# Folding the value and output weights of an attention block into one product per head, and mixing each image's context with 32-column products

## The reference: what is computed

```python
# layer 0, per image; n = 4096 pixels, four memory keys and values
xn = x / norm * g * C ** 0.5                  # norm over the channels
q, k, v = split(einsum('bchw,oc->bohw', xn, w_qkv))
k = concat([mk, k]); v = concat([mv, v])
q = softmax(q, axis=-2) * dh ** -0.5          # over the 32 channels of a head
k = softmax(k, axis=-1)                       # over the pixels
context = einsum('bhdn,bhen->bhde', k, v)
out = einsum('bhde,bhdn->bhen', context, q)
x = x + einsum('bchw,oc->bohw', out, w_out) + b_out
# layer 1
x = x + conv3x3(_gn(x), w3 * m3) + einsum(_gn(x), w1 * ~m3) + b.sum(axis=1)
```

## Time and profile before

| | before |
|---|---|
| median of three runs (lowest, highest) | 2064.62 us (2064.17, 2066.17) |
| the profiled execution, and its span | 2065.06 us, 2063.2 us |
| TensorE busy | 1913.9 us, 93% |
| VectorE busy | 1750.3 us, 85% |
| ScalarE busy, GpSimd busy | 1354.0 us, 1362.4 us |
| mean granted clock of TensorE | 0.983 |
| chain that ended last | TensorE 45%, VectorE 36%, ScalarE 12%, GpSimd 3% |

### The profile page before, as it was taken

One profiled execution on the slowest core, in us unless ns is written; L12 is line 12 of the kernel. 1 busy time (PEld: TensorE's weight loads), 2 busy tenths in 40 slices (PEclk: granted clock), 3 DMA queues, 4 the chain that ended last, 5 costly groups with the idle time before them and its releaser, 6 DMA issues.

```text
span 2063.2 us, 50607 instructions
## 1 busy us (share of the span) xinstructions
PE 1913.9 (93%) x21199; PEld 1013.4 (49%) x21199; DVE 1750.3 (85%) x3144; ACT 1354.0 (66%) x1476; POOL 1362.4 (66%) x737
## 2 busy tenths in 40 slices
PE   2889999999999999999999999999999999999996
PEld 0445445555445555444555544555544555554552
DVE  5689888888988888988888988888988888898863
ACT  2567666767667767667676766676766776766761
POOL 5566666766667766667676667676666676666762
PEclk9789999999999999999999999999999999999997
DMA  5357777887767887667787777778777778876665
GB/s 105 62 127 147 154 149 158 168 169 153 149 154 160 169 168 158 151 148 160 169 158 165 154 152 153 162 164 173 149 151 151 159 168 171 154 151 147 144 136 127
DMA packets 349427, 312.96 MB, mean 152 GB/s; under 512 B 299152, under 2 KB 299920, under 8 KB 341008
## 3 DMA queue, kind: packets, MB, share of 16 engines
q1 hardware_dynamic: 347712, 308.73, 72.1%
q10 hardware_dynamic: 1168, 0.98, 0.2%
q0 software_dynamic: 320, 0.01, 0.0%
HBM read 68.10 MB, written 67.11 MB: 66 GB/s over the span
## 4 chain that ended last, share of the span: by engine, by line
PE 45%; DVE 36%; ACT 12%; POOL 3%; issue 1%; DMA 1%; ACTq 0%; SPq 0%
PE pair_ps L765 8%; DVE km L1114 7%; DVE u L1111 7%; PE pair_ps L802 7%; PE pair_ps L745 5%; DVE image L1166 4%; DVE nrm L1101 4%; DVE parts L1101 3%; PE bank_ps L699 3%; POOL exp_kT_lo L447 3%; PE bank_ps L775 3%; PE pair_ps L768 3%; PE pair_ps L793 3%; DVE part L1100 2%; PE bank_ps L754 2%; PE bank_ps L757 2%
## 5 line engine op out<-in xcount | busy, mean ns | idle before, releaser
L802 PE MATMUL pair_ps<-replicas,w_rep 96*32 96x512 f16 x8192 | 488.9, 383 | 7.9 <-DMA replicas<-yg_lo 7.9
L444 POOL TENSOR_TENSOR u_lo<-u,u_hi 128x1024 f16<-128x1024 f32 x128 | 269.9, 2144 | 270.3 <-ACT u_hi L551 270.3
L447 POOL TENSOR_TENSOR exp_kT_lo<-exp_kT,exp_kT_hi 128x1024 f16<-128x1024 f32 x128 | 300.2, 2354 | 178.9 <-ACT exp_kT_hi L560 178.8
L802 PEld LDWEIGHTS pair_ps<-replicas,w_rep 96*32 96x32 f16 x8192 | 205.8, 96 | 263.2 <-issue 77.8
L450 POOL TENSOR_TENSOR u_lo<-exp_q,u_hi 128x1024 f16<-128x1024 f32 x128 | 272.7, 2143 | 88.8 <-ACT u_hi L566 85.3
L1166 DVE SCALAR_TENSOR_TENSOR image<-pair_ps,image 128x512 f32<-128x512 f32 x256 | 172.5, 682 | 123.5 <-PE pair_ps L802 119.8
L440 POOL TENSOR_SCALAR u<-image,st 128x1024 f32<-128x1024 f32 x128 | 187.4, 1475 | 109.2 <-DVE st L1065 109.2
L551 ACT ACTIVATE u_hi<-u 128x1024 f16<-128x1024 f32 x128 | 130.8, 1045 | 173.3 <-DVE u L1111 173.1
L557 ACT ACTIVATE exp_kT<-pair_ps,zcol 128x1024 f32<-128x1024 f32 x128 | 141.0, 1102 | 144.0 <-PE pair_ps L745 144.0
L566 ACT ACTIVATE u_hi<-exp_q 128x1024 f16<-128x1024 f32 x128 | 135.3, 1057 | 137.1 <-DVE exp_q L1153 130.5
L536 ACT ACTIVATE exp_kT<-u,zcol 128x1024 f32<-128x1024 f32 x128 | 146.0, 1143 | 93.2 <-POOL u L440 92.2
(11 more groups left out here) (179 smaller groups left out, 4716.5 us busy)
## 6 DMA issues: line engine op xcount, KB each, us to landing
image<-in_x SPq DMA_DIRECT2D x256, 256.0 KB, 4.8
out<-image SPq DMA_DIRECT2D x512, 128.0 KB, 2.2
replicas<-yg_hi SPq DMA_DIRECT2D x256, 165.0 KB, 3.9
replicas<-yg_hi SPq DMA_DIRECT2D x256, 107.2 KB, 5.1
replicas<-yg_lo SPq DMA_DIRECT2D x128, 165.0 KB, 4.4
replicas<-yg_lo SPq DMA_DIRECT2D x128, 107.2 KB, 3.8
uT_hi<-u_hi SPq DMA_TRANSPOSE x128, 3.4
uT_lo<-u_lo SPq DMA_TRANSPOSE x128, 3.4
```

The costliest lines, as they stand in the source:

```text
L444: pool.tensor_tensor(px(UL, v), px(U, v), px(UH, v), ALU.subtract).then_inc(ul_ready, 1)
L447: pool.tensor_tensor(KL[:, v % 2], KT[:, v % 2], KH[:, v % 2], ALU.subtract).then_inc(kl_ready, 1)
L802: mm = pe.matmul(conv_ps[32 * r:32 * r + 32, j % 2], w_rep[0:32 * SLOTS, tap, r], rep[:, j * ROWS + dy:(j + 1) * ROWS + dy, dx:dx + SIDE], ...
```

## The change

Per image: `weigh_context` no longer scales; it sums z, copies the context and takes the reciprocal. `turn_context` transposes the unscaled context and the unscaled `pk`. `value_context` and `mask_context` are gone. `mix_weights` is now eight products: for each head 32 columns of the turned context with `value_out[:, h]`, and 32 of the turned memory exponentials with `memory_out[:, h]`, each pair into its quarter of the bank. `split_mix` scales by 1/z while it splits. `AT_sb` is now the same buffer as `A_sb`.

Set-up: `value_out` and `memory_out` are made by two products of `wo_heads` (the output weights, block by head, times `DH ** -0.5`) with the value weights and with `mv` (`fold_values`), after the first image's last norm sums; VectorE copies them out right after `norm_guard(0)`. ScalarE permutes the weights instead of VectorE; `x_seed` and `x_scale` no longer stand behind that. The convolution weights are taken out of PSUM by ScalarE after `norm_power(0)`, rounded after the last `high_u(0)`, and split by VectorE after `rows_q(0)`; they are replicated by SP after the second step and not before the first. SP issues image 1 only when image 0 has arrived. VectorE makes the memsets of `spread` and `minus_max`.

```diff
@@ sync
-            for k in range(PRELOADED):
-                load(k, 0)
-                load(k, 1)
+            load(0, 0)
+            load(0, 1)
+            for h in range(2):
+                sp.wait_ge(x_in[h][0], at_load(0))
+            load(1, 0)
+            load(1, 1)
...
-                if s == 0 and after_first is not None:
-                    after_first()
+                if s == 1 and after_second is not None:
+                    after_second()
@@ gpsimd
-            make(pool.memset(spread[:], 0.0))
+            pool.wait_ge(setup_dve, BIASES_READY)
...
-            make(pool.memset(minus_max[:], 0.0))
@@ scalar
+                if first(s):
+                    act.wait_ge(setup_pe, TAPS_TURNED)
+                    act.activation(taps32[:, 0:8], conv_ps.rearrange("p k (t o) -> p (k t) o", o=P), ACT.Copy,
+                                   scale=W_SCALE).then_inc(setup_act, 1)
...
+                if first(s) and v == UNITS - 1:
+                    act.wait_ge(setup_act, TAPS_KEPT)
+                    act.activation(w_hi, taps32[:, 0:TAPS], ACT.Copy).then_inc(setup_act, 1)
...
-            act.wait_ge(setup_pe, 1)
-            for t in range(0, TAPS, 4):
...
+            act.wait_ge(weights_in, 16 * WEIGHT_DMAS)
+            act.activation(perm_qkv, raw_qkv.rearrange("p t (i r) -> p t r i", r=RES), ACT.Copy).then_inc(setup_act, 1)
+            act.activation(perm_w1, raw_w1.rearrange("p (i r) -> p r i", r=RES), ACT.Copy).then_inc(setup_act, 1)
+            act.activation(perm_w3, raw_w3.rearrange("p (i r t) -> p t r i", r=RES, t=TAPS), ACT.Copy).then_inc(setup_act, 1)
@@ tensor
+            def fold_values():
+
+                pe.wait_ge(setup_dve, HEADS_READY)
+                heads = wo_heads.rearrange("p h o -> p (h o)")
+                pe.matmul(pair_ps[0][:, 0:BANK], perm_qkv[:, 2].rearrange("p r i -> p (r i)"), heads, start=True, stop=True)
+                pe.wait_ge(col_in, 16 * COL_DMAS)
+                pe.matmul(pair_ps[0][0:MEM, BANK:2 * BANK], mv[:], heads, start=True, stop=True).then_inc(setup_pe, 1)
...
                 if first(s) and v == 0:
-                    pe.wait_ge(setup_dve, SETUP_READY)
-                    pe.wait_ge(const_made, POOL_STEPS)
+                    pe.wait_ge(setup_dve, PRODUCTS_READY)
+                    pe.wait_ge(setup_act, TAPS_KEPT)
+                    pe.wait_ge(const_made, SPREAD_MADE)
...
             def turn_context(ps):
-                pe.transpose(ps[:, 0:P], A_sb[:, 0:P], ident[:])
-                pe.transpose(ps[0:MEM, P:2 * P], A_sb[:, P:P + MEM], ident[:]).then_inc(mix_pe, 1)
-
-            def value_context(ps):
-                pe.matmul(ps[:, 0:P], wqkvT[:, 2], AT_sb[:], start=True, stop=False)
-                pe.matmul(ps[:, 0:P], mvT[0:MEM], pkT_sb[0:MEM], start=False, stop=True).then_inc(mix_pe, 1)
+                pe.transpose(ps[:, 0:P], A_sb[:], ident[:])
+                pe.transpose(ps[0:MEM, P:2 * P], pk[:], ident[:]).then_inc(mix_pe, 1)
 
             def mix_weights(ps):
-                pe.matmul(ps[:, 0:P], ctxT_sb[:], woT[:], start=True, stop=True).then_inc(mix_pe, 1)
+
+                for h in range(HEADS):
+                    q = slice(DH * h, DH * h + DH)
+                    pe.matmul(ps[q, 0:P], AT_sb[:, q], value_out[:, h], start=True, stop=False)
+                for h in range(HEADS):
+                    q = slice(DH * h, DH * h + DH)
+                    mm = pe.matmul(ps[q, 0:P], pkT_sb[:, q], memory_out[:, h], start=False, stop=True)
+                mm.then_inc(mix_pe, 1)
@@ vector
+                if first(s):
+                    dve.wait_ge(setup_pe, FOLDED)
+                    dve.tensor_scalar(value_out[:].rearrange("p h o -> p (h o)"), pair_ps[0][:, 0:BANK], gcol[:], None, ALU.mult)
+                    make(dve.tensor_copy(memory_out[0:MEM].rearrange("p h o -> p (h o)"), pair_ps[0][0:MEM, BANK:2 * BANK]))
...
             def weigh_context(s, ps):
-                did = chain(mix_dve, s, 9, 0)
-                did(dve.tensor_tensor(z[:, 0:1], ps[:, P:P + 1], pk_sum[:], ALU.add))
-                did(dve.reciprocal(z[:, 1:2], z[:, 0:1]))
-                did(dve.tensor_scalar(A_sb[:, 0:P], ps[:, 0:P], z[:, 1:2], None, ALU.mult), wait=False)
-                did(dve.tensor_scalar(A_sb[:, P:P + MEM], pk[:], z[:, 1:2], None, ALU.mult), wait=False)
+                did = chain(mix_dve, s, 7, 0)
+                did(dve.tensor_tensor(z[:, 0:1], ps[:, P:P + 1], pk_sum[:], ALU.add), wait=False)
+                did(dve.tensor_copy(A_sb[:], ps[:, 0:P]))
+                did(dve.reciprocal(z[:, 1:2], z[:, 0:1]), wait=False)
...
-            def mask_context(s, ps):
-                dve.tensor_tensor(ctxT_sb[:], ps[:, 0:P], head_mask[:], ALU.mult).then_inc(mix_dve, 1)
-
             def split_mix(s, ps):
-                did = chain(mix_dve, s, 9, 7)
-                did(dve.tensor_copy(MT_h[:], ps[:, 0:P]))
-                did(dve.tensor_tensor(MT_l[:], ps[:, 0:P], MT_h[:], ALU.subtract), wait=False)
+                did = chain(mix_dve, s, 7, 5)
+                did(dve.tensor_scalar(MT_h[:], ps[:, 0:P], z[:, 1:2], None, ALU.mult))
+                did(dve.scalar_tensor_tensor(out=MT_l[:], in0=ps[:, 0:P], scalar=z[:, 1:2], in1=MT_h[:],
+                                             op0=ALU.mult, op1=ALU.subtract), wait=False)
```

More of the change, by code:

```diff
@@ L66 @@
 SMALL_CONSTANTS = 13
-POOL_STEPS = 19
-BIASES_READY = 3
-WEIGHTS_READY = 6
+SPREAD_MADE = 16
+POOL_STEPS = 17
+BIASES_READY = 4
+HEADS_READY = 9
+PRODUCTS_READY = 10
 SETUP_READY = 15
+TAPS_TURNED = 2
+FOLDED = 3
+TAPS_KEPT = 5
+TAPS_ROUNDED = 6
 WEIGHT_DMAS = 1 + 4 * RES
@@ L138, in build @@
         qmT = sb("qmT", [P, P], BF16)
-        A_sb = sb("a_sb", [P, P + MEM])
-        AT_sb = sb("at_sb", [P, P])
+        A_sb = sb("a_sb", [P, P])
+        AT_sb = A_sb
         pkT_sb = sb("pkT_sb", [P, P])
-        ctxT_sb = sb("ctxT_sb", [P, P])
         MT_h = sb("mt_hi", [P, P], F16)
@@ L252, in px @@
             return t[:, v * UNIT:(v + 1) * UNIT]
-        def tap_ps(t, n):
-            pair = pair_ps[t // 8]
-            return pair[:, (t % 8) * P:(t % 8 + n) * P]
         def flat(t):
@@ L281, in image, with over_samples @@
             return B[buffer_of(sample)]
-        def over_samples(step, after_first=None):
+        def over_samples(step, after_second=None):
             def known(s):
@@ L437, in _ @@
                                         channel_multiplier=1))
+            assert made == SPREAD_MADE
+            make(pool.affine_select(out=minus_max[:], in_=minus_max[:], compare_op=ALU.not_equal, fill=-1.0,
+                                    base=0, pattern=[[-4, BLOCKS], [-1, HEADS], [0, DH]], channel_multiplier=1))
+            assert made == POOL_STEPS
             def group_norm_x(s, v):
@@ L457, in low_y @@
                 pool.tensor_tensor(inner(LO, v), rows(px(YG, v)), inner(HI, v), ALU.subtract).then_inc(lo_odd, 1)
-            make(pool.memset(minus_max[:], 0.0))
-            make(pool.affine_select(out=minus_max[:], in_=minus_max[:], compare_op=ALU.not_equal, fill=-1.0,
-                                    base=0, pattern=[[-4, BLOCKS], [-1, HEADS], [0, DH]], channel_multiplier=1))
-            assert made == POOL_STEPS
             def step(p, a, c, e):
@@ L533, in _ @@
             act.wait_ge(setup_dve, BIASES_READY)
+            act.activation(idle[:, 0:1], zcol[:, 0:1], ACT.Copy)
             def square(s, v):
@@ L686, in turn_weights @@
             def turn_weights():
-                for t in range(3):
-                    turn(conv_ps[:, 0, t * P:(t + 1) * P], perm_qkv[:, t].rearrange("p r i -> p (r i)"))
-                turn(conv_ps[:, 0, 3 * P:4 * P], raw_out)
-                turn(conv_ps[0:MEM, 1, 0:P], mv[:])
+                pe.wait_ge(setup_act, 1)
+                for t in range(2):
+                    turn(pair_ps[0][:, t * P:(t + 1) * P], perm_qkv[:, t].rearrange("p r i -> p (r i)"))
+                last = turn(pair_ps[0][:, 3 * P:4 * P], raw_out)
+                last.then_inc(setup_pe, 1)
+                pe.wait_ge(setup_act, 3)
                 for t in range(TAPS + 1):
                     src = perm_w3[:, t] if t < TAPS else perm_w1
-                    last = turn(tap_ps(t, 1), src.rearrange("p r i -> p (r i)"))
+                    dst = conv_ps[:, t // 4, (t % 4) * P:(t % 4 + 1) * P] if t < 8 else pair_ps[1][:, (t - 8) * P:(t - 7) * P]
+                    last = turn(dst, src.rearrange("p r i -> p (r i)"))
                 last.then_inc(setup_pe, 1)
+            def fold_values():
[4 more added lines that the diff above has]
+                pe.matmul(pair_ps[0][0:MEM, BANK:2 * BANK], mv[:], heads, start=True, stop=True).then_inc(setup_pe, 1)
             def norm_sums(s, v, ps):
@@ L701, in norm_sums @@
                 mm.then_inc(norm_sum, 1)
+                if first(s) and v == UNITS - 1:
+                    fold_values()
             def broadcast(ps, v, done):
@@ L761, in queries @@
```

(18 more changed lines are left out.)

90 lines of the change are left out of this document (43 added, 47 removed).

## The result

The changed kernel takes **2030.45 us** (median of 4 runs, 2029.53 to 2030.79); the kernel before, beside it on the same chip, 2065.39 us (2064.17 to 2067.15). The ratio is 0.9829, 95% interval 0.9812 to 0.9846: faster by 34.9 us, or 1.7%. Forecast were 2026.9 us and 37.8 us of gain.

The account below looks back on a forecast made before the run. Bound by a chain of waits changing engines, with TensorE's piece before `finish(3)` shortened: 31 images x 0.87 = 27 us plus 10.8 at the start, 37.8 off 2065.06, gave 2027.3, as a median 2026.9 us; range 2018 to 2044.

Parts of the forecast that it names:

- Term 1: VectorE before the first broadcast: z to cast takes 0.48 instead of 0.96 us; TensorE could use 0.47, gain 0.47 per image.
- rival B: Second operation of `split_mix` held while GpSimd runs `low_q`, 0.8 us per image: 2052 us; chance 0.11 together with the page's pace.
- Term 2: TensorE between norm sums and dense products: without `value_context`, 0.83 us shrinks to about 0.33, gain 0.5 per image.
- Term 3: `mix_weights`: eight products take 0.5 us instead of 0.42 for one, costing 0.08; VectorE hears of the end 0.1 later.
- Term 4: VectorE behind the mix: `mask_context` going gives nothing; scaling in `split_mix` adds 0.12, by which `soften(2)` was early.
- The set-up, 11.5: Program start: `x_seed` runs at once, first square at 23.7 instead of 35.24 us, gain 11.5; 6 if weights come at 26.4.
- The wait for the fold, -0.7: Set-up, VectorE after `norm_guard(0)`: waiting for the folded product sticks out of a 2.8 us cover by 0.3 to 2; 0.7 taken.
- The splitting moved, at no cost: Set-up: splitting convolution weights, some 3 us of VectorE, is covered by its 3.49 us wait behind image 1's statistics.
- A: `mix_weights`: 16 short pairs are paced at 0.055 us each, 0.88 in all, so 0.46 gained per image: 2040 us; chance 0.20.
- the page's pace: `mix_weights`: 81 ns a pair by the Trainium skill, 1.30 us for 16, near 2052 us; chance 0.11 together with B.
- C: `mix_weights`: the eight products run one after the other, 3.4 us, each image loses 2.0: slower, 2117 us; chance 0.04.
- D: Set-up gives little (late weights, the fold), 6 or less instead of 10.8: 2032 us; chance 0.62 together with the forecast.

Follow-up runs that it names:

- weigh_as_before: Changed kernel, but `weigh_context` scales again and `split_mix` copies and subtracts without scaling, the eight products kept: 2030.66 us, ratio 0.9832.
- scale_one_then_wait: Changed kernel, but GpSimd scales one unit of the next image, then waits until `parts` is done before the other three: 2016.02 us, ratio 0.9759.
- loads_not_held: Changed kernel, but SP issues the load of image 1 without waiting for image 0: 2036.84 us, ratio 0.9863.
- eight_twice: Changed kernel with the eight products of `mix_weights` issued twice, same result: 2043.11 us, ratio 0.9892.
- image_as_before: Changed kernel's set-up, but each image mixed as in the kernel before, with nothing folded: 2051.5 us, ratio 0.9931.
- waits_as_before: Changed kernel with TensorE's seven swapped pairs of waits put back in the order of before: 2031.8 us, ratio 0.9839.

## Why the prediction was right, and where it was not

The sign and the range held, and so did the mechanism of two larger terms, `value_context` and the set-up; the gain was 34.9 us where 37.8 were forecast. That the sum came so near is in part luck, since errors cancel. The new mix gave 21 us instead of 27: its first term is nearly void, and cheaper products fill only a part of that hole. The other 13.9 us, where 10.8 were forecast, hold about 1.3 us of the swapped waits, which were not in the sum, and a start that gave some 2 us more than forecast.

- *Term 1, VectorE before the broadcast, +0.47.* **Wrong, this is the step that failed.** The count of instructions held (0.47 us from z to the cast), but the cast was priced at its old 0.41 although it moved to another time. There GpSimd's scaling is under way, and the cast takes 0.84. Of 0.47 remain 0.06. The runs show what stood in its place: `parts` comes 0.54 us after the end of GpSimd's third scaling, with the short `weigh_context` and with the old one (the same time in `weigh_as_before`), and 14.4 us are gained when GpSimd waits (`scale_one_then_wait`). The rows to see it were there: the operation behind the cast was read as held by GpSimd (1.58 against 0.75) in rival B, and not asked of the cast. In its own words, "TensorE no longer idle before the first broadcast" did not come true (0.42).
- *Term 2, `value_context`, +0.5.* Right: 0.33 us between the norm sums and the dense products (0.32 from 993.57 to 993.89), and 0.49 per image when two such products are put back.
- *Term 3, eight products, -0.08, and 0.1 for VectorE.* Right in its reason and too dear in its size. Eight more cost 0.41, near the 0.46 that `denominators` gives. But the first of the eight begin beside the norm sums ahead of them, and the ring begins before the last are through. So the stretch to `mt_hi` grew by 0.03, not by 0.18, and the ring ends 0.10 earlier, counted from the start of these norm sums. Up to `mt_hi` TensorE's piece gained 0.48 where these terms gave 0.32.
- *Term 4, `split_mix` +0.12.* Its durations were right (0.35 and 0.35); rival B fell. It was costed at nothing since `soften(2)` was early by as much. It costs little: in the changed kernel `finish(3)` starts 0.09 us behind the ring's end (998.30 and 998.21), where it was 0.05 before, and the kernels with the plain `split_mix` end `soften(3)` 0.03 to 0.04 earlier.
- *Per image.* For the image traced here, 0.06 us ahead of `parts`, 0.48 from the first broadcast to `mt_hi`, 0.10 from there to the end of `soften(3)` and 0.09 behind `low_k` make 0.73; from one mix to the next it shrinks by 0.74 (from 61.37, 1019.73 to 1081.10, to 60.63, 996.52 to 1057.15). The mean over 31 images is 0.65.
- *The set-up, 11.5.* The first square came 11.1 us earlier, and the first `normalise` 12.0. The weights were there at 19.1, not 18, and the three copies took until 22.4, not 20, but GpSimd and the statistics set the pace, so neither mattered. What the forecast named as the risk (a gain of 6 us if the weights come at 26.4) is what `loads_not_held` tried: there the weights came at 26.34, and 6.4 us were lost.
- *The wait for the fold, -0.7.* Wrong: nothing. The fold took 2.1 us, between the two prices, and the cover was the time from the norm's guard to the cast, 3.51 us (42.02 to 45.53 and 30.20 to 33.71 after), which is longer than the 2.8 that were counted.
- *The splitting moved, at no cost.* Right: 2.6 us, and VectorE still waits 0.91 us behind the statistics of image 1, of 3.49.
- *Rivals.* A and the page's pace (81 ns a pair) fall by `eight_twice`: 0.026 us a record. C falls with them. B falls by the durations of `split_mix`; its mechanism, VectorE held by GpSimd, was real but struck elsewhere. D falls by the 13.9 us of `image_as_before`.

## What to carry to other kernels

When an operation is moved in time, price it anew by what the neighbouring engine does at its new place; a duration from its old place holds only there. Where one operation of a row is held, ask what the end of that row hangs on before you count what you take out of it: here it was the other engine's row. Before shortening the work ahead of a wait, look for an operation in it that takes double its free time: one wait on GpSimd gave 14 to 17 us on either kernel, the whole rewriting of the mix 21. And f32 products of 32 stationary columns onto different quarters of a bank were cheap here: eight cost 0.41 us, and less where they ran beside the products ahead of them.

## What the runs showed of the hardware

- A cast f32 to bf16 of 128x512 within SBUF is held by a GpSimd scaling that is under way: 0.84 us instead of 0.42, until that scaling ends. Even a scaling of four columns is (0.40 instead of 0.22). It goes both ways: GpSimd's own scaling takes 1.48 us on average in the changed kernel and 1.22 with the wait. By the Trainium skill, SBUF — State Buffer, on the shared port pair, whichever of the two engines comes first has the pair for its whole instruction, and VectorE's two-port operations and those with two SBUF inputs take part (the latter against a GpSimd operation that reads SBUF). The rows agree: the operation with two SBUF inputs takes 1.57 us beside GpSimd and 0.75 without, the one with one of its inputs in PSUM 0.35 as forecast. That the cast runs in a two-port mode no row shows.
- Eight f32 products of 32 stationary and 128 moving columns (16 records) take 0.41 us (`eight_twice`), and start 0.01 us behind the start of products that the program puts ahead of them (994.99 and 994.98). By the Trainium skill, TensorE: Matmul & The Clock Gate, "Back-to-back issue gap", a stream of loads and products of 128 columns takes 81 ns a pair, by which 16 pairs are estimated at 1.30 us; the runs disagree for this form.
- ScalarE's copy that permutes 128x1152 elements within SBUF takes 2.23 us, 1.9 ns a column, where its plain copy of 128x1024 out of PSUM in the same set-up takes 1.00, 1.0 ns a column, and its rounding of 128x1152 within SBUF, which permutes nothing, 1.15.
- The step from the end of GpSimd's `low_k` to TensorE's first product behind it takes 0.05 us in the changed kernel and 0.14 with TensorE's seven pairs of waits in the other order (`waits_as_before`); why, no run shows.
